# Splitting the 512-column projections of a retention and feed-forward kernel into halves of 256 columns

## What is computed

```python
def attn(x):                                  # x: [8, 512, 256] float32
    q1, k1 = rotary((x @ Wq), (x @ Wk))       # 4 heads of 64
    v = x @ Wv                                # 4 heads of 128
    o = chunk_retention(q1 * 64**-0.5, k1, v, gamma)   # per chunk: (q k^T * D) v + q S;  S = gC S + k^T v
    o = rmsnorm(o, gn_weight)
    return (o * silu(x @ Wg)) @ Wo

def ffn(x):
    return (silu(x @ wg.T) * (x @ wu.T)) @ wd.T   # w = integers / 127

x = layernorm(x + attn(x))
x = layernorm(x + ffn(x))
```

## Time and profile before

| | |
|---|---|
| median of 3 runs | 449.84 us (449.81 to 450.4) |
| profiled execution | 450.35 us, of which 448.6 us are the span from the first to the last instruction |
| mean granted clock of TensorE | 0.996 of full speed |
| PE busy | 433.9 us (97%), 3288 matmuls |
| PEld busy | 392.7 us (88%) |
| DVE, ACT, POOL busy | 307.4, 268.5, 239.1 us |
| DMA | 18.45 MB, mean 41 GB/s |

### The profile page before, as it was taken

How to read it: one execution, slowest core, us unless ns; L and a number is a source line. 1 busy time by engine, 2 the same in 40 slices (tenths; PEclk the granted TensorE clock), 3 DMA queues, 4 the chain that set the end, 5 groups by cost and what they waited for, 6 DMA issues and landing times.

```text
span 448.6 us, 10332 instructions
## 1 busy us (share of the span) xinstructions
PE 433.9 (97%) x3288; PEld 392.7 (88%) x3288; DVE 307.4 (69%) x785; ACT 268.5 (60%) x794; POOL 239.1 (53%) x381
## 2 busy tenths in 40 slices
PE   7998999999999999999999999999999999999993
PEld 3777889999999999999999999999999999999983
DVE  4988455686666677666768667678766667865764
ACT  5678666655655566655566556556665556665541
POOL 2644255645655466454666436665565536554564
PEclk9999999999999999999999999999999999999998
DMA  7901010020100101020010101001010100100011
GB/s 244 373 17 49 0 40 10 1 61 13 61 12 22 38 12 58 12 58 11 7 52 12 58 12 58 0 12 58 12 58 12 35 1 12 37 14 12 14 38 38
DMA packets 15932, 18.45 MB, mean 41 GB/s; under 512 B 1440, under 2 KB 13728, under 8 KB 15904
## 3 DMA queue, kind: packets, MB, share of 16 engines
q1 hardware_dynamic: 15904, 18.09, 12.4%
HBM read 13.89 MB, written 4.19 MB: 40 GB/s over the span
## 4 chain that ended last, share of the span: by engine, by line
PE 89%; DVE 4%; issue 2%; ACT 2%; DMA 1%; POOL 1%; SPq 0%; POOLq 0%; ACTq 0%; DVEq 0%
PE b_rows L395 45%; PE b_ffn L395 18%; PE b_head L488 6%; PE b_state L395 3%; PE b_head L458 3%; PE b_head L461 3%; PE b_turn L408 3%; PE b_turn L514 3%; PE b_ffn L477 2%; DMA wf_int<-in_w_proj 1%; POOL h_lo L1229 1%; ACT wf_int L816 1%; DVE y L1062 1%; DVE rot_s L966 1%; DVE rot_c L959 0%
## 5 line engine op out<-in xcount | busy, mean ns | idle before, releaser
L1229 POOL TENSOR_TENSOR h_lo<-wf_int,h_hi 128x256 fp32r<-128x256 f32 x96 | 71.1, 740 | 60.5 <-ACT h_hi L806 59.8
L395 PE MATMUL b_ffn<-x1T_hi,wf_hi 128*128 128x256 f32 x384 | 92.8, 279 | 0.1
L395 PE MATMUL b_ffn<-x1T_lo,wf_hi 128*128 128x256 f32 x384 | 91.9, 277 | 0.0
L395 PE MATMUL b_rows<-wp_hi,xT_hi 128*128 128x512 f32 x186 | 78.8, 424 | 1.3 <-ACT v_sb L719 1.3
L395 PEld LDWEIGHTS b_ffn<-x1T_hi,wf_hi 128*128 128x128 f32 x384 | 72.1, 188 | 3.4 <-DVE x1T_lo L1041 0.5
L395 PEld LDWEIGHTS b_ffn<-x1T_lo,wf_hi 128*128 128x128 f32 x384 | 72.1, 188 | 2.8
L1254 POOL TENSOR_TENSOR ve<-mv,eps 128x1 f32<-128x1 f32 x64 | 14.0, 219 | 111.8 <-DVE mv L1083 103.6
L395 PE MATMUL b_rows<-wp_hi,xT_lo 128*128 128x512 f32 x186 | 73.5, 395 | 0.0
L395 PE MATMUL b_rows<-wp_lo,xT_hi 128*128 128x512 f32 x186 | 73.4, 394 | 0.0
L770 ACT ACTIVATE sq<-b_head 128x128 f32<-128x128 f32 x128 | 35.5, 277 | 58.6 <-PE b_head L488 55.6
L1074 DVE TENSOR_TENSOR z<-b_rows,x_sb 128x256 f32<-128x256 f32 x32 | 13.6, 424 | 66.8 <-PE b_rows L395 66.8
(11 more groups left out here) (102 smaller groups left out, 1073.0 us busy)
## 6 DMA issues: line engine op xcount, KB each, us to landing
xT_raw<-in_xT SPq DMA_DIRECT2D x16, 256.0 KB, 3.0
x_sb<-in_x SPq DMA_DIRECT2D x16, 256.0 KB, 2.7
out<-wf_int SPq DMA_DIRECT2D x32, 128.0 KB, 1.7
wf_int<-in_w_ffn SPq DMA_DIRECT2D x6, 384.0 KB, 7.1
wf_int<-in_w_proj SPq DMA_DIRECT2D x6, 256.0 KB, 4.7
rope_sb<-in_rope SPq DMA_DIRECT2D x4, 256.0 KB, 6.3
wo_raw<-in_w_o SPq DMA_DIRECT2D x1, 512.0 KB, 7.0
gn_sb<-in_gn SPq DMA_DIRECT2D x1, 0.5 KB, 6.4
```

What stands on the lines that cost most here:

```text
L395: mm = pe.matmul(dst, a, b, start=(i == 0 and j == 0 and not begun), stop=(i == n - 1 and j == len(passes) - 1 and not more), skip_group_c ...
L1229: pool.tensor_tensor(h_lo[:, ring, hb], h_full[:, u], h_hi[:, ring, hb].bitcast(F32), ALU.subtract).then_inc(h_split[j], 1)
```

## The change

A projection (other than slot 0's) no longer goes through `split_product` but through a new function, `projection_passes(dst, stat, mov, whole)`. It makes the same list of six passes in the same order. The first `whole` of them are issued over all 512 columns as before. The others are issued twice with 256 columns: first all of them for columns 0 to 255, then all of them for columns 256 to 511. `whole` is 1 for c=0, 0 for c=1 and 3 for c=2. Sums, operands, banks, waits and signals are the same; the signal stands on the last half.

```diff
+            def projection_passes(dst, stat, mov, whole):
+                passes = [(sh if st == 0 else sl, mh if mt == 0 else ml)
+                          for (sh, sl), (mh, ml) in zip(stat, mov) for st, mt in ((0, 0), (0, 1), (1, 0))]
+                n = len(passes)
+                for i in range(whole):
+                    a, b = passes[i]
+                    pe.matmul(dst[:], a, b, start=i == 0, stop=False, skip_group_check=True)
+                for cols in (slice(0, 256), slice(256, 512)):
+                    for i in range(whole, n):
+                        a, b = passes[i]
+                        mm = pe.matmul(dst[:, cols], a, b[:, cols], start=i == 0, stop=i == n - 1,
+                                       skip_group_check=True)
+                return mm
...
                 else:
-                    mm = split_product(dst[:], stat, mov)
+                    mm = projection_passes(dst, stat, mov, (1, 0, 3)[c])
                 mm.then_inc(done, 1)
```

## The result

The changed kernel takes **453.8 us** (median of 7 runs, 453.22 to 455.51) where the kernel before takes 449.84 (7 runs, 449.56 to 452.18). The ratio over all runs is 1.0082, with a 95% interval of 1.0071 to 1.0093 (the two medians alone would give 1.0088). The prediction, 447.4 with a range up to 448.8, has the wrong sign: 2.4 us were to be gained, and some 4 us were lost.

The account below looks back on a forecast made before the run. TensorE's own pace was taken to bound the kernel: 40 + 27 + 22 = 89 ns per slot over 26 slots give 2.3 us, plus 0.1 from early slots, 2.4 off 449.84: 447.4 us, range 446.7 to 448.8.

Parts of the forecast that it names:

- What bounds the kernel: From 62 to 413 us only TensorE's own pace counts; 100 ns less there are 100 ns less at the end.
- The price of a split, 6.7 ns,: fp32r products on TensorE: one of 512 columns takes 233.3 ns, two of 256 take 226.7, so 6.7 ns gained.
- c=1, 40 ns,: Projection behind the down projection, all six products split: 1400 ns become 1360, 40 ns gained per slot.
- c=2, 22 ns,: Projection behind transposes, three whole and six halves: 22 ns gained per slot, ends 15 and 25.
- c=0, 27 ns,: Projection behind four plain fp32 transposes, one whole and ten halves: 36 ns less about 9, 27 gained per slot.
- Rival C: Projections: a fee per product, halves every 119 ns, 62 ns more per slot, 451.4 us; chance slower 0.04, within 0.2% 0.04.
- Rival B: Behind fp32 work halves gain nothing: c=0 and c=2 give 0, only c=1 its 40 ns; 448.8 us, chance 0.05.
- Rival D: In the loop, a late ACT or DVE result makes TensorE wait and eats the gain; 449.8 us, chance 0.03.
- Rival E: The four-slot loop outgrows TensorE's instruction store and code is fetched again (q8); +3 to +15 us, less 2.4; chance 0.02.

Follow-up runs that it names:

- e1: Against the kernel before, only c=1 is split, all six products; c=0 and c=2 keep six whole: 449.34 us against 450.3, ratio 0.9978.
- e10: Against the kernel before, only c=1 is changed: two whole products, then eight halves: 449.69 us against 450.8, ratio 0.998.
- e7: The changed kernel with no whole product left in c=0, c=1 or c=2, all halves: 447.75 us against 450.55 before, ratio 0.9936.
- e3: Against the kernel before, only c=2 is split (three whole, six halves): 450.41 us against 450.3, ratio 1.0001, not told from none.
- e4: The changed kernel without its c=0 part: c=0 six whole, c=1 none, c=2 three: 449.04 us against 450.3 before, ratio 0.997.
- e5: The changed kernel with four whole products in c=0 instead of one: 448.87 us against 450.55 before, ratio 0.9964.
- e8: The changed kernel with two whole products in c=0 instead of one: 448.22 us against 450.55 before, ratio 0.9956.
- e2: Against the kernel before, only c=0 is split (one whole, ten halves): 454.16 us against 450.3, ratio 1.009.
- e11: The changed kernel with one whole product put back at the head of c=1: 452.35 us against 450.8 before, ratio 1.0036.
- e12: The changed kernel with c=0 and c=1 all halves and one whole product in c=2: 447.65 us against 450.8 before, ratio 0.9935.
- e6: The changed kernel with five whole products in c=0 instead of one: 453.78 us against 450.55 before, ratio 1.0073.
- e9: Against the kernel before, only c=1 is changed: one whole product, then ten halves: 451.64 us against 450.8, ratio 1.0029.

## Why the prediction was wrong, point by point

- **What bounds the kernel** was right. TensorE alone sets the time from 62 to 413 us, before and after, and a nanosecond lost there is one at the end.
- **The price of a split, 6.7 ns,** was right: e1 gives 40 ns for six, e10 27 for four, e7 107 for eighteen less the tails.
- **c=1, 40 ns,** was right (e1). **c=2, 22 ns,** was right (e3: 20).
- **c=0, 27 ns,** is the step that failed. As the prediction put it, "three kinds of products (gate/up, down, output) with different tiles, into halves and into the start of a bank, have the same 113 ns", and so the halves would have it too. 113.3 ns is not the pace of a 256-column fp32r product but one of two, and which one holds depends on what stands ahead in the stream. The term is not 27 ns gained but 207 lost (e4's -60 against the change's +147), since with one whole product in c=0 up to 56 products behind it are 4.4 ns later each, 46 of them outside c=0. In place of 89 ns gained per slot, 147 were lost.
- The reading that led there: the pace was taken from streams behind six wholes and behind none. Neither is the changed kernel's case, one whole, and its value was taken as lying between two that happened to agree. The drain at 418 us, in the same trace, had 117.7 ns and would have shown that the pace isn't fixed. What the prediction held against its own forecast, that no row had a slice of a 512-wide row of `wp`, didn't matter: e7's projections are nothing but such slices and go at 113.
- **Rival C** had a price near the measured one by accident (119 ns assumed, 117.8 measured; from 116.7 on a split loses), and with it the sign; its 451.4 us are 2.4 short of the 453.8. The sign of being wrong that the prediction gave for it, halves that start every 117 ns or more, did show. But it was a fee of the halves alone. By it e1 would have been slower, and it was faster. Its mechanism falls, and its 62 ns per slot were too few, since it left out the products that the change doesn't touch, 34 of the 56.
- **Rival B** falls: c=2 gains, and c=0 does too wherever the pace is 113 (e5, e7, e8). **Rival D** falls: no new wait. **Rival E** falls: no q8 in the loop's repeats, and e7, whose loop has four more split products per slot than the change, is among the fastest.
- On the page of the Trainium skill ("TensorE: Matmul & The Clock Gate", section on the back-to-back issue gap), whose formula for the gap between two products speaks against splitting: in e7 all 18 splits together gain 107 ns per slot where it would give 2.5 ns of loss each. The change is slower, as that formula would have it, but not for that reason.

## What stays open

The runs show that whole products swap the pace, and where; they don't show what inside TensorE keeps it, nor what sets it when a stream begins. I have no account for three things. One is why a whole swaps the pace behind the transposes of q and k and in mid-stream, but not behind those of y in slots 7 to 31. Another is why slots 1, 2 and 6 of the changed kernel go at 113 behind the one whole of c=0; in e2 and e11, whose c=0 is the same, slot 6 goes at 118, so the place in the program doesn't decide it. The third is why some streams go at 118 without a whole: the drain's at 418 us, and the one around c=0 in slot 5 of e12. The count of wholes is a rule that held in slots 7 to 31 of e5, e6 and e8 to e11, not a mechanism. No run changed the number or the timing of the fp32 products ahead of a stream, which would be the next step. Each kernel has the trace of one execution, so whether the pace of a stream can differ from one execution to the next isn't shown either.

## What to carry to other kernels

Read the pace of a product in every stream of the trace, not in one: if two values occur anywhere, it is not a property of the product, and a change of what stands at a stream's head can move all that is behind it. Then undo the change part by part before believing in a sum: e1 and e3 showed that two of three parts did what was expected. Here the best versions have no whole product where the swap acts (e7: 0.64% faster than before, 2.8 us); what a mixed stream does in another kernel has to be measured there.

## What the runs showed of the hardware that was not expected

- A stream of 256-column fp32r products, each with its own weight load, at a granted clock of 1.00, runs at either 113.3 or 117.8 ns from start to start, without any wait recorded, for the same operands, and keeps its pace over 50 and more products (slots 6 and 7 of the changed kernel).
- One 512-column product in mid-stream swaps the two (from 113 to 118 in e9, from 118 to 113 in e11), two in a row don't change it (e10), six leave 118 at 118 (e2). 512-column products have the same mean, some 232 ns, in both (c=1 of the kernel before and of e2).
- Two kernels that differ only in whether one product of each c=0 is split differ by 1.1% of the whole time (e5 and e6, 448.87 and 453.78 us).
